# Softmax groups of 16 chunks in place of 8, and a ring of edge rows in which values lie on older keys

## The reference, cut to what matters

```python
# x: 6250 x 256;  4 heads of 64;  8 relations;  4 node types
q_att = einsum('nhd,rhde->rnhe', q, relation_att)       # per relation
v_msg = einsum('nhd,rhde->rnhe', v, relation_msg)
attn_score = sum(q_att[etype, dst] * k[src], axis=-1)   # per edge and head
score = attn_score * (relation_pri[etype] / SQRT_DK)
m = segment_max(score, dst)
ex = exp(score - m[dst])
alpha = ex / segment_sum(ex, dst)[dst]
agg = segment_sum(alpha[..., None] * v_msg[etype, src], dst)
x = x + gnn(layernorm(x)) + mix(layernorm(x))           # mix: linear attention over all nodes, then an MLP
...                                                     # then a feed-forward on the half with the highest router weight
```

## Time and profile before

| | |
|---|---|
| median of 3 runs | 2380.79 us (2377.87 to 2383.92) |
| span of the profiled execution | 2514.6 us; no other time is known of that execution |
| busy over the span | PE 81%, DVE 70%, ACT 59%, POOL 47% |
| gathers, keys, values (L2248) | 880 DMAs, first at 554.1 us, last at 2023.1 us |
| scores (L1883) | 220, first at 564.5 us, last at 2048.4 us |

### The profile page before, as it was taken

How to read it: one execution, slowest core, us unless ns; L and a number is a source line. 1 busy time by engine, 2 the same in 40 slices (tenths; PEclk the granted TensorE clock), 3 DMA queues, 4 the chain that set the end, 5 groups by cost and what they waited for, 6 DMA issues and landing times.

```text
span 2514.6 us, 38612 instructions
## 1 busy us (share of the span) xinstructions
PE 2034.6 (81%) x10630; PEld 1506.8 (60%) x10630; DVE 1762.5 (70%) x4682; ACT 1483.8 (59%) x4969; POOL 1180.2 (47%) x1207
## 2 busy tenths in 40 slices
PE   6999998985888888888888888888888774812999
PEld 5865554544666666666666666666666553611666
DVE  8867765544788888888888888888888664626121
ACT  6755554553667677777667676777767574620222
POOL 0033334335556565656655566556656413661231
PEclk9999999987999999999999999999999887965999
DMA  5868878986788887778878888888878837840110
GB/s 186 312 239 320 326 312 286 357 344 200 234 262 245 262 254 253 251 256 253 258 238 262 258 254 266 255 256 259 264 244 245 192 79 243 278 163 31 48 58 33
DMA packets 272145, 587.07 MB, mean 233 GB/s; under 512 B 45595, under 2 KB 186145, under 8 KB 265275
## 3 DMA queue, kind: packets, MB, share of 16 engines
q0 software_dynamic: 93936, 387.70, 47.1%
q1 hardware_dynamic: 177995, 196.89, 24.2%
HBM read 407.88 MB, written 176.99 MB: 233 GB/s over the span
## 4 chain that ended last, share of the span: by engine, by line
PE 46%; DVE 18%; ACT 14%; issue 10%; another core or an unknown queue 6%; DMA 4%; DVEq 1%; SPq 1%; POOL 0%; POOLq 0%; ACTq 0%
ACT arena L1267 10%; PE bank L904 7%; PE bank L739 7%; PE bank L872 4%; PE bank L893 4%; PE bank L1061 4%; PE bank L1072 4%; PE bank L718 3%; PE bank L587 2%; DMA arena<-chunk_rel 2%; DVE arena L1873 2%; DVE arena L1883 2%; PE bank L725 1%; DVE arena L1959 1%
## 5 line engine op out<-in xcount | busy, mean ns | idle before, releaser
L2248 POOL DMA_INDIRECT arena<-table,arena x880 | 862.9, 981 | 616.6 <-PE bank L904 360.7
L1267 ACT ACTIVATE arena<-arena 128x64 f32<-128x64 f32 x3520 | 857.3, 339 | 0.0
L904 PE MATMUL bank<-arena 128*128 128x260 f32 x1760 | 494.0, 420 | 58.7 <-issue 26.4
L904 PEld LDWEIGHTS bank<-arena 128*128 128x128 f32 x1760 | 342.9, 206 | 159.8 <-issue 65.3
L1873 DVE TENSOR_TENSOR arena<-bank,arena 128x512 f32<-128x512 f32 x440 | 300.3, 684 | 112.5 <-remote 52.5
L893 PE MATMUL bank<-arena 128*128 128x256 bf16 x2640 | 339.0, 279 | 11.5 <-issue 10.2
L893 PEld LDWEIGHTS bank<-arena 128*128 128x128 bf16 x2640 | 257.5, 100 | 73.4 <-issue 14.2
L1883 DVE TENSOR_REDUCE arena<-arena 128x16 f32<-128x1024 f32 x220 | 265.7, 1208 | 11.9 <-issue 0.5
L587 PE MATMUL bank<-arena 128*128 128x128 f32 (+1 forms) x643 | 127.2, 306 | 149.9 <-issue 47.6
L739 PE MATMUL bank<-arena 64*128 64x512 f32 x832 | 211.1, 624 | 22.3 <-DVE arena L1609 11.1
L872 PE MATMUL bank<-arena 128*128 128x256 f32 (+1 forms) x800 | 198.1, 393 | 7.5 <-issue 7.5
(11 more groups left out here) (310 smaller groups left out, 2978.2 us busy)
## 6 DMA issues: line engine op xcount, KB each, us to landing
arena<-q_parts SPq DMA_DIRECT2D x440, 192.0 KB
arena<-chunk_rel SPq DMA_DIRECT2D x220, 128.0 KB
arena<-table,arena POOLq DMA_INDIRECT x880
node_rows<-arena SPq DMA_DIRECT2D x24, 512.0 KB, 7.2
xl_and_sum<-arena SPq DMA_DIRECT2D x8, 1536.0 KB
arena<-in_x SPq DMA_DIRECT2D x12, 512.0 KB, 8.6
xn<-arena SPq DMA_DIRECT2D x12, 512.0 KB, 8.6
xT<-arena SPq DMA_DIRECT2D x12, 512.0 KB, 8.1
```

What stands on the lines that cost most here:

```text
L904: ins = TE.matmul(bank[b][:, 0:AW], lhsT=so[p % 2][:, c % 2, j, :], rhs=ring[:, c % NR, j, EX0:EX0 + AW], start=j == 0, stop=j == HALF - 1)
L1267: ins = A.activation(seg, seg, ACT.Copy, scale=rows[:, EX0 + h:EX0 + h + 1])
L2248: G.indirect_dma_start(ring[:, i % NR, j, :], None, d_tab_rows[0:N * R, :], bass.IndirectOffsetOnAxis(ap=idxE[:, g, j, c:c + 1], axis=0)). ...
```

## The change

Groups are of `GC` = 16 chunks (8 pairs): 28 groups (27 full ones and one of 4 pairs) in place of 55. Rows of a group are 32 a head in place of 16, so its tiles have 128 partitions in place of 64, and the chain over them 136 elements in place of 72. The lags grow with the group: 9, 10 and 11 pairs in place of 5, 6 and 7.

The ring is laid out anew. A place is 260 columns. A pair takes two neighbouring places: its keys lie in the one, its values in the next, with their weights now behind them. As places are taken in steps of 7 around 18, keys of pair `p + 13` are written onto values of pair `p`, and values of pair `p + 5` onto keys of pair `p`. So the gather of pair `p` waits for the scatter of pair `p - 13` and for the score of pair `p - 5`. The copy of the weights into the ring goes in as many pieces as the places of a group ask for. Registers of places are still loaded for every 8 chunks (`PLACES`). The marks of a group have 2 buffers in place of 3 and are loaded at the fifth pair of a group (`MARKS_AT`).

```diff
-GC = 8
+GC = 16
 SG = -(-NCH // GC)
-NPAIR = SG * GC // 2
+NPAIR = -(-NCH // 2)
...
-WEIGH_LAG, SUM_LAG, ADD_LAG = 5, 6, 7
+WEIGH_LAG, SUM_LAG, ADD_LAG = PG + 1, PG + 2, PG + 3
+PLACES = 8
+MARKS_AT = 4
...
-NR, NRB, NQ3, NFR = 20, 3, 3, 3
-
-AHEAD = 5
+NRB, NQ3, NFR = 3, 3, 2
+RING_PAIRS = 10
+KEYS_LIFE, VALUES_LIFE, RING_STEP = 5, 13, 7
+RING_BLOCKS = KEYS_LIFE + VALUES_LIFE
...
-    ring = view(lo, NR * HALF * KV, "p (c j n) -> p c j n", c=NR, j=HALF); lo += NR * HALF * KV
+    ring = view(lo, LANES * LANE, "p (l b n) -> p l b n", l=LANES, b=RING_BLOCKS + 1); lo += LANES * LANE
...
+    def block_of(p):
+        return p * RING_STEP % RING_BLOCKS
+
+    def keys_of(c):
+        p, i = divmod(c, 2)
+        return ring[:, i * HALF:(i + 1) * HALF, block_of(p), H:AW]
+
+    def values_of(c, j):
+        p, i = divmod(c, 2)
+        return ring[:, i * HALF + j, block_of(p) + 1, :]
+
+    def rows_of_pair(p, lane):
+        at_ = lo_ring + lane * LANE + block_of(p) * AW + H
+        return arena[:, at_:at_ + KV]
+
+    def pieces_of(g):
+        pieces = []
+        for p in range(g * PG, last_of(g) + 1):
+            if pieces and block_of(p) > block_of(p - 1):
+                pieces[-1].append(p)
+            else:
+                pieces.append([p])
+        return pieces
...
-            for part in range(2):
-                lo_, rows = (g * GC + part * GC // 2) % NR, ROWS // 2
-                ins = A.copy(ring[:, lo_:lo_ + GC // 2, :, EX0:C].rearrange("p c j h -> p (c j) h"),
-                             bank[GB][:, C_EX:C_EX + H * ROWS].rearrange("p (h r) -> p r h", h=H)[:, part * rows:(part + 1) * rows, :])
+            for pairs_ in pieces_of(g):
+                first, n = pairs_[0], len(pairs_)
+                b0, r0 = block_of(first) + 1, (first - g * PG) * LANES
+                ins = A.copy(ring[:, :, b0:b0 + (n - 1) * RING_STEP + 1:RING_STEP, C:AW].rearrange("p l n h -> p n l h"),
+                             bank[GB][:, C_EX:C_EX + H * ROWS].rearrange("p (h r) -> p r h", h=H)[:, r0:r0 + n * LANES, :].rearrange("p (n l) h -> p n l h", n=n))
             ins.then_inc(ex_put, 1)
...
         for p in range(NPAIR):
-            if p >= NR // 2:
-                b, k = psum.at("sum", 2 * (p - NR // 2) + 1)
+            if p >= VALUES_LIFE:
+                b, k = psum.at("sum", 2 * (p - VALUES_LIFE) + 1)
                 G.wait_ge(full[b], k)
-            elif p >= AHEAD:
-                G.wait_ge(scored, p - AHEAD + 1)
+            if p >= KEYS_LIFE:
+                G.wait_ge(scored, p - KEYS_LIFE + 1)
...
-            if at_ == 3 and g + 2 < SG:
-                load_marks(g + 2)
+            if at_ == MARKS_AT and 1 <= g and g + 1 < SG:
+                load_marks(g + 1)
```

More of the change, by code:

```diff
@@ L86 @@
 ACC_PARTS = 7
-EX0 = C - H
+LANES = 2 * HALF
+LANE = (RING_BLOCKS + 1) * AW
+assert RING_STEP * VALUES_LIFE % RING_BLOCKS == 1
 def tiles_of(g):
@@ L421, in build @@
     runA = view(lo, H * SLOTS, "p (h s) -> p h s", h=H)[0:1]; lo += H * SLOTS
-    carry = [[view(lo + (2 * i + q) * H * ROWS, H * ROWS, "p (h r) -> p h r", h=H)[0:1] for q in range(2)] for i in range(2)]; lo += 4 * H * ROWS
+    carry = [view(lo + q * H * ROWS, H * ROWS, "p (h r) -> p h r", h=H)[0:1] for q in range(2)]; lo += 2 * H * ROWS
     q3r = [view(lo + i * 2 * 3 * C // 2, 2 * 3 * C // 2, "p (c s n) -> p c s n", dt=bf16, c=2, s=3) for i in range(NQ3)]; lo += NQ3 * 3 * C
@@ L903, in scatter @@
                 for j in range(HALF):
-                    ins = TE.matmul(bank[b][:, 0:AW], lhsT=so[p % 2][:, c % 2, j, :], rhs=ring[:, c % NR, j, EX0:EX0 + AW], start=j == 0, stop=j == HALF - 1)
+                    ins = TE.matmul(bank[b][:, 0:AW], lhsT=so[p % 2][:, c % 2, j, :], rhs=values_of(c, j), start=j == 0, stop=j == HALF - 1)
                 ins.then_inc(full[b], 1)
@@ L1263, in weigh @@
             for j in range(HALF):
-                rows = ring[:, c % NR, j, :]
+                rows = values_of(c, j)
                 for h in range(H):
-                    seg = rows[:, C + h * DK:C + (h + 1) * DK]
-                    ins = A.activation(seg, seg, ACT.Copy, scale=rows[:, EX0 + h:EX0 + h + 1])
+                    seg = rows[:, h * DK:(h + 1) * DK]
+                    ins = A.activation(seg, seg, ACT.Copy, scale=rows[:, C + h:C + h + 1])
             ins.then_inc(weighed, 1)
@@ L1982, in vector_program @@
                 score(p)
-            if (a + 1) % PG == 0 and 0 <= a + 1 < NPAIR:
-                load_places((a + 1) // PG)
+            if 2 * (a + 1) % PLACES == 0 and 0 <= a + 1 < NPAIR:
+                load_places(2 * (a + 1) // PLACES)
             if p + 2 < NPAIR:
@@ L1999, in vector_program @@
         V.wait_ge(mix_base, MG)
-        t = step(V.tensor_scalar(rden, accv[:, :, 0:H], 0.5, None, ALU.max))
+        t = step(V.tensor_scalar(rden, accv[:, :, C:AW], 0.5, None, ALU.max))
         V.wait_ge(dve_step, t)
@@ L2007, in vector_program @@
                 if tile % GT < GT - 1:
-                    part = accv[:, tile, H:AW].rearrange("p (h d) -> p h d", h=H)
+                    part = accv[:, tile, 0:C].rearrange("p (h d) -> p h d", h=H)
                     ins = V.tensor_tensor(out=part, in0=part, in1=rden[:, tile, :].unsqueeze(2).to_broadcast([P, H, DK]), op=ALU.mult)
```

42 lines of the change are left out of this document (21 added, 21 removed).

## The result

The changed kernel takes **2368.98 us** (median of 12 runs, 2362.93 to 2376.8), the kernel before, timed beside it, 2380.11 us (12 runs). The ratio is 0.9954, 95% interval 0.9938 to 0.997: 11 us faster, where 58 were forecast. The time lies at the far end of the range, nearer to the rival "no change" (2381) than to the mix rival (2351).

A forecast was written before the change was run, and what follows sets the result against it. It saw no single bound, but PE and DVE at 85% waiting for each other, notably at group steps. Group steps -73 and lags +12 gave -61, x 0.947 = -58: 2323 us from 2380.79; forecast 2298 to 2345, range 2284 to 2370.

The forecast's parts named there:

- no change: Rival: other waits of ACT and PE fill the freed time and only the drain is left, 2381 us; chance 0.10.
- mix rival: Rival: the mix part's chain across PE, ACT and DVE waits longer, taking back 30 us, 2351 us; chance 0.15.
- Group steps: Edge stage, 53 groups to 27: 84 us less on DVE, 66 on PE, not added; 73 us taken.
- clock rival: Rival: fewer group waits keep PE off half clock, up to 37 us more gain, 2288 us; chance 0.07.
- Lags: End of the edge stage: four more pairs weighed in the drain, 15.7 us, less 3.4 of adds; net +12 us.
- Ring: Gathers start one pair later, 13.0 us ahead of use, with about 5.9 us of cover left; cost 0.
- slower: late gathers: Rival: pairs land later than 13.0 us after their gather's start and stretch the pace, 2402 us; chance 0.08.
- Width: Group steps on 128 partitions: chain 0.52 us longer a group on DVE, turns 0.1 on PE, scans and shifts unchanged.
- The scaling by 0.947: Sum made against the profiled span of 2514.6 us, brought over to the runs' median of 2380.79: -61 became -58 us.
- What would show it: Signs: 28 scans, middle pace 6.3 us, idle time ahead of `turn_carry` near half, drain near 45 us.

The follow-up runs named there:

- dup_scans: The kernel before with two more scans of 64x128 on DVE in every group, results unused; ratio 1.0091 (1.0064 to 1.0118), long session.
- half_steps2: The kernel before with the group steps of every second group left out, result then not the reference's, in a short session; ratio 0.981 (0.9783 to 0.9837).
- mix1 kernels: The kernel before and the changed kernel, each with the mix part's second half one half step later; 2398.02 and 2378.27 us, ratios 1.0098 and 1.0015.
- nrb4_chunk: The changed kernel with a fourth buffer for relations and gathers that wait per chunk; ratio to the kernel before 1.0208 (1.0168 to 1.0249), long session.
- before_mix1: The kernel before with the second half of the mix part one half step later; ratio 1.0098 (1.0066 to 1.0131), short session.
- lead3: The kernel before with each gather held back by one pair (waiting for the scatter of p - 9); ratio 0.9981 (0.9954 to 1.0008), long session.
- ring_marks3: The changed kernel with groups of 8 chunks, the old lags and marks loaded at step 3; ratio to the kernel before 0.9987 (0.9952 to 1.0021).
- after_third: The changed kernel unaltered, against the kernel before, in the third session (long); ratio 1.0113 (1.0067 to 1.0159).
- half_steps: The kernel before with the group steps of every second group left out, result then not the reference's, in a long session; ratio 0.9909 (0.9869 to 0.9948).
- after_again: The changed kernel unaltered, against the kernel before, in the second session (long); ratio 1.0093 (1.0066 to 1.012).
- after_fourth: The changed kernel unaltered, against the kernel before, in the fourth session (short); ratio 0.9965 (0.9943 to 0.9987).

## Why the prediction was wrong

**Group steps: the worth was wrong, not the price.** The step that failed is "Where PE had been last, 66 counts, where DVE, 84. I take 73 us". The freed time was there, 82 us on DVE and 73 on PE. I took it as removed from a path on which always one of the two is last. dup_scans and half_steps2 measured it: 17 to 23 us for 39 to 43 us put in on DVE, 45 us for 101 us (DVE) and 72 us (PE) taken out. About half shows. With the width, which those 73 us included, the term is -45 + 26 = -19 us in a short session. (The price on PE also left out `turn_scores`: its 45 turns carry the helper's line L587 and take 0.27 us each, with no wait, about 7 us for the groups removed.)

**Where the other half went.** The traces show three places where idle or slow time grew; how the lost half divides among them no run shows. First, waits across PE, ACT and DVE around the mix part (37 us more in the pair of mix1 kernels), which is the mechanism of the rival "less: the mix chain", priced there at 30 us. Second, DVE's waits for the loads of relations (28 us more in that pair), which no rival had. No run in a short session took this wait away, so it stays open whether these loads hold the pace or only stand where DVE would wait anyway. Third, the clock, with the sign turned round: the clock rival had fewer waits give fewer falls. By the clock records of the traces, between 700 and 1900 us PE is at half clock (1.2 GHz) for 116 to 137 us in the nine kernels with the steps of 55 groups (dup_scans, with its added work, 150), and for 140 to 175 us in nine of those with 28 (nrb4_chunk 208); in short sessions alone, 116 (before_mix1) against 140 to 164. Of the 28 falls in the changed kernel, 19 have as PE's longest idle time just ahead a wait at L616. The waits ahead of `turn_carry` that went were 2.1 us on average and 6.3 at most (before_mix1); the ones at L616 are longer, 4.5 us on average and 6.0 at most. In the mix1 pair 24 us more at half clock are up to 12 us of lost work, an estimate. That long waits cause the falls, and not the other way round, was argued and not shown.

The Trainium skill, "TensorE: Matmul & The Clock Gate", Part 1, on which that rival leaned, has the gate close once PE has been idle. The falls behind the waits at L616 agree with it. What I had made of it did not hold: I counted the group waits that vanish, and not the waits that grow in their place.

**Lags: right, as far as the runs can tell.** +12 forecast; the drain went from 29.3 to 42.9 us, 13.6 more where 15.7 were forecast, and the runs gave 8 and 10 us in all, each uncertain by 10 us or more. ACT's weighing sets it, as the second window shows (38.36 of 42.90 us busy).

**Ring: right.** lead3 and ring_marks3 cost nothing, and DVE's products wait for no gather in the middle of the stage (L1903 above: all of its 57.9 us but 0.7 are for PE). By the DMA packets of the changed kernel's trace, gathers land 5 us ahead of use in the median and 2 us in the tightest hundredth, 5.9 forecast. Two errors partly cancel in that: gathers start 13.7 us ahead (13.0 forecast), and the last of a pair lands 4.9 us behind its issue, not 3.3. The new wait for the score of p - 5 was met 21 times, 20.1 us in all, and did no harm that the runs show. The rival "slower: late gathers" did not happen; in after_third, a long session, the margin is 6.4 us in the median and never under 2.7.

**Width: the steps' lengths right, their cost too small.** The chain grew by 1.75 - 1.17 = 0.58 us for 0.52 forecast; scans and shifts together by 0.05, so partitions are nearly free. That is 27 x 0.63 = 17 us of DVE's time, yet the kernel lost 17 to 35 us by it, and 19 by the pace. What costs beyond DVE's own steps wasn't found; the marks and copies that also differ were not tried apart.

**The scaling by 0.947.** It took a trace of one kind of session for a copy of the other, only longer. It isn't: the same edit gave -23 us (half_steps) where before takes 2520, and -45 us where it takes 2375, and the whole change +24 and +28 us there against -8 and -11 here. A span 5.6% over the runs was a warning that what bounds the kernel may differ, and I used it as a factor.

**What would show it.** 28 scans: yes. A pace of 6.3: 6.28, yet against a pace before of about 6.3 too. (before_mix1 has 6.42 and is 23 us slower than the kernel before, 0.11 us a pair; the 6.3 is an estimate from that.) The idle time ahead of `turn_carry` near half: 23.0 of 44.8, yes. Drain near 45: 42.9. The mix rival's sign, more idle time at the transposes: yes. So all the signs of the forecast came true and the time did not: each showed that a part had changed, and none that the end had waited for it.

**What stays open.** In long sessions the parts don't add up: 23 us less, 6 more for ring and lags, 14 to 26 for the width would give about the same time, but the changed kernel is 24 to 28 us slower. There the pace itself does not gain: 6.60 and 6.65 us in after_third and after_again, 6.60 to 6.67 in the three traces of the kernel before. In those traces many waits have no releaser ("remote" or "issue"), so the rest isn't placed; late gathers are ruled out by the margin above. What makes a session long wasn't found.

## What to carry to other kernels

Where two engines at 85% wait for each other, the time that an edit frees on both is not the time that it saves: put a known amount of work in at that place (two spare scans did it here) and see what share of it the kernel's time shows, before you multiply the count of removed steps by their length. When waits go from one place, name the next chain of fixed latency, here the mix part, and the next load in line, here the relations, and ask how much of the freed time they can take back. Price the kept steps by a run too: twice as wide, they cost more here than their added length. And when a profiled execution is some per cent longer than the runs, don't scale it; that length is a sign that another condition may bound the kernel.

## What was unexpected of the hardware

The same kernel takes 2375 us in one session and 2520 in another, while single instructions last the same (the score 1221 ns in the median in both). DVE is busy 5.3 us a pair in after_third and in after_fourth alike, so its difference lies in waits; 41 us more lie in the end stage (389 us after the reciprocal in after_fourth, 430 in after_third). PE is busy 5.5 us a pair against 5.4. One numbered chip was seen in both conditions, so it isn't simply a slow chip. An edit can be a gain in one and a loss in the other.

Twice the partitions cost a scan 8 and 15 ns (L1891 to L1921, 401 to 409; L1893 to L1923, 419 to 434), while 64 more elements along the free axis cost another 135 ns (L1901 to L1931, 288 to 423).
